# Attention blocks with the two pairs of maxima products apart on TensorE

## The reference

```python
q = proj(layernorm(x), Wq, bq)          # 8 heads of 16
k = proj(ctx, Wk, bk); v = proj(ctx, Wv, bv)
scores = einsum('bhqd,bhkd->bhqk', q, k) / sqrt(16)
attn = softmax(scores, axis=-1)          # 512 x 512 for each head
out = einsum('bhqk,bhkd->bhqd', attn, v)
x = x + tanh(g_xattn) * out
# then layernorm, rmsnorm, router, 8 experts (top 2), a shared expert, added to x
```

## Time and profile before

| | |
|---|---|
| median of three runs | 1387.68 us |
| the profiled execution | 1386.7 us, span 1384.8 us, mean granted TensorE clock 0.983 |
| TensorE busy | 1288.3 us (93%) |
| VectorE busy | 975.1 us (70%), of it 615.0 in 512 row maxima |
| ScalarE busy | 871.8 us (63%), of it 552.4 in 1024 exponentials |
| GpSimd busy | 861.5 us (62%) |
| span of the attention turns with every part in them | about 130 to 806 us |

### The profile page before, as it was taken

The page is one execution under the profiler, slowest core; times in us unless marked ns, Lnnn a source line. Parts: engine busy times, 40 slices in busy tenths (PEclk is TensorE's granted clock), DMA queues, the critical chain, the costliest instruction groups (busy, mean ns, idle before and its releaser), DMA issues.

```text
span 1384.8 us, 34397 instructions
## 1 busy us (share of the span) xinstructions
PE 1288.3 (93%) x12274; PEld 682.2 (49%) x12274; DVE 975.1 (70%) x1661; ACT 871.8 (63%) x1720; POOL 861.5 (62%) x1267
## 2 busy tenths in 40 slices
PE   2899999999999999999999989799999999999997
PEld 0233333333333333333333323587788888888886
DVE  5989889999999998989999877457654333333332
ACT  2488888888888888888888768333334333333332
POOL 8647777678787878877887643442114555555553
PEclk7799999999999999999999999999999999999999
DMA  7677887778888888788888773676555998885665
GB/s 187 185 197 227 224 241 220 207 227 214 201 223 207 213 218 227 191 222 210 218 217 221 162 185 90 161 161 149 127 175 105 214 216 193 178 189 110 108 110 81
DMA packets 167522, 256.65 MB, mean 185 GB/s; under 512 B 31717, under 2 KB 65132, under 8 KB 167358
## 3 DMA queue, kind: packets, MB, share of 16 engines
q1 hardware_dynamic: 149102, 217.08, 59.0%
q0 software_dynamic: 18256, 37.38, 14.9%
HBM read 141.06 MB, written 112.27 MB: 183 GB/s over the span
## 4 chain that ended last, share of the span: by engine, by line
PE 61%; DVE 12%; issue 10%; DMA 7%; POOL 3%; ACT 3%; SPq 2%; POOLq 1%; DVEq 0%; ACTq 0%
PE m_banks L956 21%; PE bank L913 12%; PE bank L882 10%; DVE row_max L1129 8%; PE m_banks L860 7%; PE bank L838 3%; PE bank L888 3%; DMA arena<-parts_q 2%; PE bank L844 2%; ACT arena L1413 2%; DMA arena<-ht_d 1%; POOL xs L780 1%; PE bank L978 1%; SPq L458 1%; PE bank L869 1%
## 5 line engine op out<-in xcount | busy, mean ns | idle before, releaser
L1129 DVE TENSOR_REDUCE row_max<-m_banks 128x2 f32<-128x1024 f32 x512 | 615.0, 1222 | 76.1 <-PE m_banks L860 67.9
L1413 ACT ACTIVATE arena<-bank 128x512 f32<-128x512 f32 x1024 | 552.4, 606 | 73.4 <-PE bank L882 71.9
L882 PE MATMUL bank<-arena 112*32 112x512 bf16 x4096 | 336.2, 382 | 6.6 <-ACT arena L1413 3.2
L913 PE MATMUL bank<-arena 128*32 128x512 f32 x2048 | 280.2, 598 | 0.4 <-ACT arena L1421 0.3
L882 PEld LDWEIGHTS bank<-arena 112*32 112x32 bf16 x4096 | 114.7, 95 | 266.0 <-ACT arena L1413 132.4
L792 POOL DMA_INDIRECT out<-xs,ids x71 | 112.3, 1582 | 173.4 <-ACT xs L1495 135.7
L860 PE MATMUL m_banks<-arena 48*128 48x512 bf16 x1024 | 177.4, 393 | 39.6 <-DVE row_max L1129 25.7
L956 PE MATMUL m_banks<-w_ring,h_hi 128*128 x568 | 183.0, 403 | 0.0
L1484 ACT ACTIVATE arena<-m_banks 128x256 f32<-128x256 f32 x103 | 39.5, 384 | 186.9 <-PE m_banks L956 186.9
L860 PEld LDWEIGHTS m_banks<-arena 48*128 48x128 bf16 x1024 | 40.4, 93 | 175.2 <-DVE row_max L1129 79.9
L1337 DVE TENSOR_TENSOR arena<-arena,m_banks 128x256 f32<-128x256 f32 x71 | 29.9, 421 | 116.5 <-ACT arena L1484 116.5
(11 more groups left out here) (182 smaller groups left out, 1999.9 us busy)
## 6 DMA issues: line engine op xcount, KB each, us to landing
arena<-parts_k SPq DMA_DIRECT2D x128, 192.0 KB
arena<-parts_q SPq DMA_DIRECT2D x128, 192.0 KB
parts_k<-arena SPq DMA_DIRECT2D x64, 256.0 KB, 6.6
parts_q<-arena SPq DMA_DIRECT2D x64, 256.0 KB, 5.1
pv_d<-arena SPq DMA_DIRECT2D x32, 512.0 KB, 4.3
split_d<-staged SPq DMA_DIRECT2D x30, 512.0 KB, 9.1
w_ring<-split_d SPq DMA_DIRECT2D x60, 256.0 KB, 3.9
arena<-in_w SPq DMA_DIRECT2D x36, 256.0 KB, 8.4
```

The lines of the kernel that those rows point to most:

```text
L882: last = nc.tensor.matmul(out[c, :], k_stack[b % 3][0:SHIFTED, h, kt * P + c.start:kt * P + c.stop], q_stack[b % 3][0:SHIFTED, h, :], star ...
L913: last = nc.tensor.matmul(pv_ps[2 * DH * j:2 * DH * (j + 1), :], v_ones[b % 3][:, kt, GROUP * g + j, :], probs[pair % 3][:, j, :], start=( ...
L1129: nc.vector.reduce_max(pair, m_ps[(STEPS * b + u) // 2 % M_PAIRS], AX_X).then_inc(s_mx, 1)
L1413: nc.scalar.activation(probs[group % 3][:, j, :], bank_of["scores", b, s], ACT.Exp, scale=float(DH) ** -0.5).then_inc(s_exp, 1)
```

## The change

In each block of a turn the second M moves from behind the first M to behind the second pair of E; V moves from the end of the block to just behind the first M; and the extras of a block (token transpose, logits, projection) now stand behind the second M. In letters, with [x] for an extra and (T) for the transpose of the maxima:

- before: E E M M [x] E E (T) V
- after: E E M V E E M [x] (T)

The programs of the other engines, `EVAC_AT` among them, stay as they are.

```diff
                         exp_scores(i, s + 1)
                     if is_b(i + 1):
                         max_scores(i + 1, s)
+                    if s == 0 and is_b(i - 1):
+                        values(i - 1, STEPS // GROUP - 1)
+                    if s and is_b(i):
+                        values(i, s // GROUP - 1)
+                    if is_b(i):
+                        exp_scores(i, s + 2)
+                        exp_scores(i, s + 3)
+                    if is_b(i + 1):
                         max_scores(i + 1, s + 2)
                     if s == TURN_TOKENS_AT and is_b(i - 3):
                         turn_tokens(i - 3)
@@
                     if s in PROJECT_AT and is_b(i + PROJECT_AT[s][0]):
                         project(i + PROJECT_AT[s][0], PROJECT_AT[s][1])
-                    if is_b(i):
-                        exp_scores(i, s + 2)
-                        exp_scores(i, s + 3)
                     if s + 3 == MAX_AT[1] and is_b(i):
                         turn_maxima(i, 1)
                     if s + 3 == MAX_AT[0] and is_b(i + 1):
                         turn_maxima(i + 1, 0)
-                    if s == 0 and is_b(i - 1):
-                        values(i - 1, STEPS // GROUP - 1)
-                    if s and is_b(i):
-                        values(i, s // GROUP - 1)
```

## The result

The changed kernel takes 1625.35 us in the median of four runs (1624.76 to 1630.41), the kernel before beside it 1386.54: a ratio of 1.172, 95% interval 1.169 to 1.176. The forecast was 1612, with a range of 1550 to 1680. The profiled execution has a span of 1623.0 us and a mean granted clock of 0.976, where it had 1384.8 and 0.983.

The account below looks back on a forecast made before the run. TensorE was taken as the bound, VectorE close behind; the new order makes TensorE and ScalarE alternate. 26 turns by 7.5 us (195), three without tokens (21) and the last turns (9) add 225 to 1386.7: 1612 us, range 1550 to 1680.

Parts of the forecast that it names:

- the relay: TensorE and ScalarE work in turns behind extras: the next block's E waits for an exponential queued behind the projection's evacuation.
- The walk through the banks: One full turn followed step by step through the three-bank rotation: 33.46 us against 25.96, 7.5 us more.
- The four legs of the walk: Stretches from evacuation at s = 24 to 28, to copy at 8, to token copy, to evacuation at 24: 5.28, 11.53, 4.73, 11.92 us.
- The two unknown steps: V and E directly behind a single M, not in the trace: taken as 0.32 us, bounds 0.21 and 0.53.
- The wait of V for the copy: At s = 4 and 20 V waits for ScalarE's copy of values: starts 6.01 instead of about 5.5, and at 6.39 us.
- The turns behind turn 29: Turns 29, 30 and 31 at the end, with fewer extras: some 4.5, 3 and 1.5 us more, together 9.
- Drains only: Rival: only tile-form changes on TensorE cost, 0.26 us in each of 8 blocks, 2.1 a turn: 1440 us; chance 0.07.
- Faster: Rival: VectorE is fed evenly and the 25.7 us of M waiting for row maxima go: 1362 us; chance 0.05.
- Clock: Rival: TensorE's 1.5 us pauses lower the clock in half of four stalled blocks a turn: about 1770 us; chance 0.06.
- a granted clock below 1 in the turns: Sign named for the profile after: seeing it in the turns would make the prediction wrong.

Follow-up runs that it names:

- the split alone: Against the kernel before, only the second M of each block moved behind the second pair of E; extras and V stayed: 1410.97 us, ratio 1.016.
- the run with V late: Changed kernel, but at s = 4 and 20 V stands behind the second M again: 1638.04 us, ratio 1.173 against the kernel before.
- the run that filled the pauses: Changed kernel plus four unneeded maxima products on TensorE behind the extras of s = 8, 12 and 24: 1631.75 us, ratio 1.167 against the kernel before.
- the two filled kernels: Changed kernel with unneeded maxima products behind extras of s = 8, 12, 24 (1631.75 us), or also s = 28, with s = 12 only where tokens are (1647.8 us).
- ScalarE following: Changed kernel with ScalarE's projection evacuations moved behind exponentials 27, 31 and 11, its token copy behind 15: 1457.45 us, ratio 1.051 against the kernel before.
- the extras ahead of V: Changed kernel with the extras put back ahead of V and the second pair of E, ScalarE's order old: 1440.75 us, ratio 1.038 against the kernel before.

## Why the prediction was right, step by step

**The bound and the relay.** The walk through the banks gave 33.46 us a full turn, 30.9 without tokens and 5.28 between the evacuations; the trace has 33.44, 30.86 and 5.26. The four legs of the walk agree too: 5.28, 11.53, 4.73 and 11.92 were forecast, and between ScalarE's starts at 512.51, 517.77 and 529.31 the trace has 5.26 and 11.54, between those at 495.87, 500.59 and 512.51 it has 4.72 and 11.92. That the cause is ScalarE's place against the extras, not the split, is shown by a ladder of runs in which one thing moves at a time (shortest full turn): 25.10 before; 25.74 with the split alone; 26.94 with V in the middle too; 33.44 with the extras behind the second pair as well, the changed kernel. From there ScalarE's order alone brings it back to 27.20. Of 8.3 us, 0.6 are the split, 1.2 V (its two waits for the copy, 0.46 and 0.74, as the trace of that run has them), and 6.5 the extras. The shares hold for this order of steps only: the extras moved alone, with neither the split nor V, cost 2.7 us and not 6.5, since ScalarE then has its projection earlier.

**The constants.** Projection to evacuation 1.13, evacuation to exponential 0.59, end of an exponential to E 0.05, M to V 0.32, all read from the trace of before, held in the new order. The two unknown steps, V and E behind a single M, were taken from their nearest row and were equal to it (0.32).

**The wait of V for the copy.** It came as counted (0.46 and 0.73 us; the walk has some 0.5 and 6.39 - 5.62 = 0.77). That it would be gained back if V stood behind the second M was not claimed, and is refuted by the run with V late.

**The sum over the kernel.** 225 us forecast, 239 measured, and the 14 that lie between are the sum of a larger error and one that offsets it. The larger one is in the turns: 26 by 7.5 is 195, and they grew by 216. The walk is of an undisturbed turn, and I took it against the mean turn of before, 25.96, which holds 0.86 us of waits and transfers above the shortest, 25.10. Like against like, the growth is 8.3 us (25.10 to 33.43 for the shortest, 25.96 to 34.26 for the mean), not 7.5. What the forecast lacks is this 0.8 us for each of 26 turns, 21 us: the changed kernel has disturbances of its own, in the mean 0.82 us a turn above 33.44, and the walk had nothing for them. The other is at the end and hides a part of the first. The turns behind turn 29 grew by 8.5 us, 9 forecast; but from the last E to the end of the program it is 502.1 us, 510.7 before, 8.6 less, although nothing was changed there. This stretch lies between 503 and 514 us in the other kernels here, so it varies by as much without this change. The rest, ahead of turn 0 and in the turns without tokens, is right within 2 us. Had it stayed the same, the kernel would have taken some 1634. That 1612 came within 1% of 1625 owes this much to luck; the growth of the turn doesn't.

What the 21 us are: waits for a late q are 4.0 of them, five in all. Eight turns with a fall of the granted clock hold 19 of the 21, with 3.2 of these waits among them; so some 16 us, by this estimate, go with the falls. The longest turn (38.3 us) has 1.83 us ahead of one M and two falls. That they would be gained back by keeping the clock up is not shown: the run that filled the pauses had fewer falls and the same mean turn.

**The rivals.** Drains only: the split does cost time, but its price was mis-sized. The step that failed is "0.26 in each of 8 blocks is 2.1 us a turn"; the split alone measured 0.64 in the shortest turn and 1411 us in the kernel, not 1440. It is nearly right in the block of s = 28, too much in most others, and it leaves out the waits that the split removes. In the walk itself this error does no harm, since there each step is taken from its own row. Faster: VectorE does get its M more evenly (its row maxima hold up an M for 7.0 us with the split alone, 25.7 before), but even then the kernel is 1.6% slower. Only the variant that splits where a projection was queued behind the waiting M is not slower; there the gain is 0.4%, and the traces don't show it plainly. Clock: it dips now and then, as the range allowed for, in about ten places of some hundred stalled blocks, and not in half of them. The prediction also named a granted clock below 1 in the turns as a sign that it would be wrong. That sign did appear, and the forecast held all the same, because the falls are few; as a sign it was drawn too sharply.

**What was named to look for.** Turns of 33 us are there, and so is ScalarE idle 2.1 us ahead of lines 1397 and 1401; ahead of 1429 it is 2.05, for about 1.7 named. E waits 1.2 to 1.4 us behind each extra but the logits (1.5 forecast, and what the trace puts down is its idle time, less the matmuls' modelled ends). The experts' program is as before, and the stretch behind the attention 8.6 us shorter, as said above.

## What to carry to other kernels

When instructions move on one engine, hold the other engines' fixed programs against the new order, and write out which bank of a rotation each user takes: a consumer that keeps its old place turns a pipeline into a relay, and here moving the consumer by two places brought back 12 of the 17 points that were lost. A walk of one period with a dozen constants from the trace of before gives the new period to 0.1 us. A wait that a row names isn't a gain: ask what stands right behind it (V's 0.73 us became E's 0.72), and price a step between two tile forms in each kind of block by itself, with the waits that the new order takes away. Set an undisturbed walk against an undisturbed period of before, not against the mean.

## What the hardware showed that was not expected

The granted clock fell, to the lower of its two levels, behind pauses of TensorE of 1.26 to 1.39 us; I had looked for it behind waits near 2.9 us. In the changed kernel the stretch from 294.0 to 298.6 us has a granted clock of 0.63 in the view by stretch (length, busy us of TensorE first, then clock, DMA share, GB/s):

```profile
294.00:298.60 4.60, 4.37 (x28) 0.98 (x28) 1.48 (x2) 2.91 (x7) 3.58 (x12) 0.63 0.34 114
```

Before it TensorE had paused 1.27 us behind the tokens' transposes. The same pause came in every turn and the fall in only some of them; with about 1.0 us of filler in it, and no wait for q behind it, there was none in either of the two filled kernels. In the two kernels without the relay, ScalarE following or the extras ahead of V, the pauses are gone and the falls behind them too: their few falls in the turns stand behind waits for q of 1.9 to 5.6 us. What decides in which turn it falls is not shown here. A fall lasts some 3 to 3.5 us and makes a turn 1.3 to 2 us longer (turns of 34.8 to 35.4 us where it is the only one and no late transfer is seen).
